# The second layer norm's output turned by DMA transposes of fp16 parts, and fp16 part products for Q, K and V

## Chip, cores and metric

One core of one Trainium2 chip. The metric is the device time of one execution of the program in microseconds (us), the median of several runs. Before the change it is 1558.5 us, the median of three runs (1556.65 to 1559.55).

## What is computed

A macaron block in float32 on 2 sequences of 2048 tokens with 256 features: half a feed-forward block, attention, half a feed-forward block, each behind a layer norm without weights.

```
h(x)  = relu(s0 * [x,-x] @ W0) * 2        # W0 entries +1 or -1, 512 x 1024
        relu(s1 * h @ W1) * 2             # 1024 x 1024, +1 or -1
        s2 * h @ W2                       # 1024 x 256, +1 or -1
x = x + 0.5 * h(layernorm(x))
x = x + attention(layernorm(x))           # 16 heads of 16, causal, then @ w_o.T + b_o
x = x + 0.5 * h(layernorm(x))
```

Inside the attention the three projections q, k and v are `layernorm(x) @ w.T` with 256 x 256 float32 weights. They are what the change is about.

## The kernel before

The 4096 tokens are cut into 8 chunks of 512. There are three phases. Phase A takes each chunk through the first feed-forward block, the second layer norm and the projections to q, k and v, which are stored to scratch in DRAM. Phase B is attention, pair of heads by pair of heads. Phase C is the output projection, the third layer norm and the second feed-forward block. The change touches phase A alone.

Every engine runs its own instruction list, written out by hand, and they meet at semaphores. An engine that waits for one semaphore holds up everything behind it in its list. In phase A one turn of the chunk loop does the following on TensorE (`chunk`, L1129):

- L1, the 1024 x 1024 layer of chunk c, tiles m = 0 to 2 (`pe_l1`, L427). Each of the 8 output tiles takes 16 matmuls of 512 columns, because the activations are kept as an fp16 high part and an fp16 low part;
- eight 128 x 128 transposes of the normalised rows of chunk c-1 (`pe_t2`, L742, by the helper `pe_transpose`, L403) into the PSUM tile `ffn_tr`;
- L1 tile m = 3;
- `pe_qk` (L748) and `pe_v` (L760) for chunk c-1: float32 matmuls of the turned rows `proj_in` with the turned weights `w_t`, 8 for Q and K with 512 columns and 8 for V with 256. The compiler emits two instructions for each float32 matmul, so the profile counts 16 and 16;
- L1 tiles m = 4 to 7, then L2 (`pe_l2`, L444, 64 matmuls of 256 columns), then L0 of chunk c+1 (`pe_l0`, L413, 32 matmuls of 512 columns).

The last chunk (c = 7) is written out apart from L1163 on. It has attention's first row-maximum items (`pe_early`, `dve_early`) put between its matmuls. `pe_qk` and `pe_v` of chunk 6 come there only after L1 and L2, and those of chunk 7 after them.

VectorE (`chunk` L964, `next_ln` L977) makes the low parts: `dve_hidden` (L509) subtracts the high part from each hidden tile. At the end of a turn it handles the 8 tiles of the next L0, the statistics of the second norm of chunk c (`dve_ln_stats(ln2, c)`), the statistics of the first norm of chunk c+2, and then finishes both norms (`dve_ln_finish`, L380), second norm first. The normalised rows are `ln2.xn` and `ln1.xn`. ScalarE makes the high parts (`act_hidden`, L493), copies the turned rows from PSUM to `proj_in` (`act_x2`, L771) and takes q, k and v out of PSUM (`act_qk` L777, `act_v` L785). `dve_qk` (L796) makes the low part of q and k.

The first norm of each chunk has already another way to the turned form: `act_x_rows` (L473) writes its fp16 high part by rows, `dve_x_rows` (L479) the low part, and `sp_turn_x` (L485) turns both with four DMA transposes issued from SyncE (SP), 128 tokens each. SP's list for phase A is at L832 to L847: in each turn it stores q, k and v of chunk c-1 and then turns the first norm's rows of chunk c+1. After chunk 3 it also loads the first two pairs of heads for phase B (`load_pair`).

GpSimd adds the output bias to the residual once `ln2.xn` is there (`add_bias`, L897).

Of the kernel before, what the change touches and what calls it, by code (L numbers as in the profile page):

```python
# [19 lines left out]
F32 = mybir.dt.float32  # L20
# [8 lines left out]
P = 128  # L29
# [16 lines left out]
QK_SCALE = 2.0 ** 3  # L46
M_SCALE = 2.0 ** 13
# [62 lines left out]
class PhaseASems:  # L110


    def __init__(self, new):
# [29 lines left out]
        self.wt = new("wt")  # L143

# [112 lines left out]
def build(nc, x, w_q, w_k, w_v, w_o, b_o, k0, k1, k2, s0, s1, s2, out):  # L257
# [8 lines left out]
    with ExitStack() as top:  # L266
# [374 lines left out]
        first_turn_after = sum(map(len, L1_FILLS[:3]))  # L641
        l2_after = sum(map(len, L1_FILLS))
        tr_after_turn = slots.index(0, first_turn_after)
# [72 lines left out]
        with ExitStack() as st:  # L716
# [13 lines left out]
            w_max = sbuf(st, "w_max", [P, 2], F32)  # L730
            w_amax = sbuf(st, "w_amax", [P, 2], F32)
            w_lim = sbuf(st, "w_lim", [P, 2], F32)
            w_pow = sbuf(st, "w_pow", [P, 2], F32)
            w_inv = sbuf(st, "w_inv", [P, 2], F32)
# [7 lines left out]
            def pe_t2(c, last=False):  # L742
                wait(nc.tensor, ln2.sem.xn, c + 1)
                if last:
                    wait(nc.tensor, sb.s_done, last_use(0, in_qk))
                pe_transpose(ln2, f.tr, se.t2_ps)

            def pe_qk(c, src, bank_free, fill=None):  # L748

                wait(nc.tensor, se.x2_t, c + 1)  # L750
                for j in range(2 * DT):
                    bank_free(j)
                    for kt in range(DT):
                        ins = nc.tensor.matmul(f.mm[:, j, :], w_t[:, j // DT, kt, j % DT * P:(j % DT + 1) * P],  # L754
                                               src[:, kt, :], start=(kt == 0), stop=(kt == DT - 1))
                    ins.then_inc(se.qk_ps, 1)
                    if fill:
                        fill()

            def pe_v(c, src, bank_free):  # L760

                for t in range(TPC):
                    if t % 2 == 0:
                        bank_free(t // 2)
                    for kt in range(DT):
                        ins = nc.tensor.matmul(f.acc[:, t // 2, t % 2 * D:(t % 2 + 1) * D], src[:, kt, t * P:(t + 1) * P],  # L766
                                               w_t[:, 2, kt, :], start=(kt == 0), stop=(kt == DT - 1))
# [3 lines left out]
            def act_x2(c, dst):  # L771
                wait(nc.scalar, se.t2_ps, c + 1)
                if dst is proj_in:
                    wait(nc.scalar, se.v_ps, c * 2)
                nc.scalar.activation(dst[:, :, :], f.tr[:, :, :], ACT.Copy).then_inc(se.x2_t, 1)

            def act_qk(c, js):  # L777
                for j in js:
                    if j == 0:
                        wait(nc.scalar, se.qk_st, c * 128)  # L780
                    wait(nc.scalar, se.qk_ps, c * 4 + j + 1)
                    nc.scalar.activation(qk_hi[:, j, :], f.mm[:, j, :], ACT.Copy,
                                         scale=qk_scale[:, j // DT:j // DT + 1]).then_inc(se.qk_hi, 1)

            def act_v(c):  # L785
                for j in range(2):
                    if j == 0:
# [4 lines left out]
                                         ACT.Copy).then_inc(se.v_ev, 1)  # L792
# [3 lines left out]
            def dve_qk(c, js):  # L796
                for j in js:
                    wait(nc.vector, se.qk_hi, c * 4 + j + 1)
                    nc.vector.scalar_tensor_tensor(out=qk_lo[:, j, :], in0=f.mm[:, j, :],
                                                   scalar=qk_scale[:, j // DT:j // DT + 1], in1=qk_hi[:, j, :],  # L800
# [3 lines left out]
            def _(sp):  # L804
# [36 lines left out]
                for i in range(QCH - 2):  # L841
                    store(1, i)
                    sp_turn_x(sp, f, i + QCH + 2)
                for i in range(2):
# [5 lines left out]
            def _(pool):  # L850
# [17 lines left out]
                pool.wait_ge(se.wmax, 2)  # L868
                nc.gpsimd.partition_all_reduce(w_amax[:, :], w_max[:, :], P, RMAX).then_inc(se.wamax, 1)
                pool.wait_ge(se.wamax, 1)  # L870
                pool.wait_ge(se.wscale, 2)
# [39 lines left out]
            def _(dve):  # L911
# [33 lines left out]
                for n in range(2):  # L945
# [15 lines left out]
                nc.vector.tensor_scalar(qk_scale[:, :], w_inv[:, :], QK_SCALE, None, ALU.mult).then_inc(se.wscale, 1)  # L961
# [15 lines left out]
                def next_ln(c):  # L977
# [4 lines left out]
                    dve_ln_finish(ln2, c, se.t2_ps)  # L982
# [3 lines left out]
                next_ln(0)  # L986
                with dve.Fori(1, NCH - 2) as c:
# [3 lines left out]
                dve_ln_finish(ln2, NCH - 2, se.t2_ps)  # L991
# [3 lines left out]
                for m in range(HT):  # L995
# [3 lines left out]
                    dve_hidden(f, c, [m], 1)  # L999
                dve_early(n)  # L1000
# [7 lines left out]
                dve_ln_finish(ln2, c, se.t2_ps)  # L1008
# [8 lines left out]
            def _(act):  # L1017
# [32 lines left out]
                act.wait_ge(se.wscale, 2)  # L1050
                act.wait_ge(se.vones, 1)
                chunk(1)
# [6 lines left out]
                act_hidden(f, c, range(0, 3), 1)  # L1059
                act_x2(c - 1, proj_in)  # L1060
                act_hidden(f, c, range(3, HT), 1)
# [3 lines left out]
                act_x2(c, proj_last)  # L1065
# [6 lines left out]
            def _(pe):  # L1072
# [56 lines left out]
                def chunk(c, first=False):  # L1129
# [15 lines left out]
                def fill_early():  # L1145
# [3 lines left out]
                    if n == tr_after_turn:  # L1149
                        wait(pe, se.x2_t, NCH - 1)  # L1150
# [14 lines left out]
                pe_l1(f, c, range(0, 3), l1_free(c, True), fill_early, fills=L1_FILLS)  # L1165
                wait(pe, sb.s_done, last_use(0, first_turn_after))
                pe_t2(c - 1)
                pe_l1(f, c, range(3, HT), l1_free(c, True), fill_early, fills=L1_FILLS)
# [359 lines left out]
```

## Time and profile before

| | us |
|---|---|
| median of three runs | 1558.5 |
| profiled execution, its own time | 1557.87 |
| profiled execution, span from first to last instruction | 1556.2 |
| TensorE busy | 1534.5 (99% of the span) |
| VectorE busy | 1121.3 (72%) |
| ScalarE busy | 840.4 (54%) |
| GpSimd busy | 193.6 (12%) |

Phase A takes from 0 to about 452 us, phase B to about 1190 us, phase C the rest. Busy time of TensorE counts overlapping matmuls once, so 99% says that it is hardly ever without work. How far apart matmuls start says how fast it works.

### The profile page before, as it was taken

The page shows a single profiled execution, that of the slowest core. Times are in us where ns is not written, and L with a number is a line of the kernel's source. Part 1 is how long each engine was busy: PE and PEld are TensorE (multiplying, and loading weights), DVE is VectorE, ACT ScalarE, POOL GpSimd, SP SyncE. Part 2 cuts the span into 40 slices and gives each one's busy share as a digit, 9 for nine tenths or more (in the row PEclk, how much of TensorE's full clock was granted, in tenths as well). Part 3 has the DMA queues.
Part 4 walks back from the last instruction along what each step waited for, and adds up shares of the span by engine and source line. Part 5 has one row for each costly group of instructions (what it writes and reads, how often), then busy time and mean ns, then how long its engine had stood idle before and what let it go on. Part 6 is the DMA issues. An engine that isn't in the chain of part 4 may idle for free.

```text
span 1556.2 us, 35447 instructions
## 1 busy us (share of the span) xinstructions
PE 1534.5 (99%) x14112; PEld 723.8 (47%) x14112; DVE 1121.3 (72%) x1616; ACT 840.4 (54%) x1703; POOL 193.6 (12%) x516
## 2 busy tenths in 40 slices
PE   6999999999999999999999999999999999999998
PEld 3555555555444333434334334333433555555554
DVE  6535543564769999999989999989996667666552
ACT  3223322322158888888888888888886222222221
POOL 4300000000111112121112212212220000000000
PEclk9999999999999999999999999999999999999999
DMA  5121023402040222211222211222220222211210
GB/s 172 28 68 54 13 68 89 113 13 67 1 116 23 63 70 62 70 43 45 61 70 63 83 54 54 67 83 69 65 76 22 82 68 74 74 53 55 81 27 14
DMA packets 146227, 96.39 MB, mean 62 GB/s; under 512 B 106544, under 2 KB 125616, under 8 KB 146096
## 3 DMA queue, kind: packets, MB, share of 16 engines
q1 hardware_dynamic: 146096, 94.54, 21.2%
q8 instruction: 94, 1.54, 0.4%
q14 instruction: 37, 0.30, 0.1%
HBM read 49.15 MB, written 37.75 MB: 56 GB/s over the span
## 4 chain that ended last, share of the span: by engine, by line
PE 97%; DVE 1%; ACT 1%; DMA 0%; issue 0%; DVEq 0%
PE ffn_mm L437 29%; PE ffn_mm L1312 18%; PE ffn_mm L1332 16%; PE ffn_mm L423 7%; PE ffn_acc L453 7%; PE ffn_acc L659 6%; PE ffn_tr L659 5%; PE ffn_mm L754 4%; PE ffn_acc L568 2%; PE ffn_acc L766 2%; DVE m_part L680 1%; PE ffn_tr L407 1%; PE ffn_tr L665 1%; PE ffn_acc L665 0%; ACT probs L1288 0%; DMA x_res<-L_attn_x 0%
## 5 line engine op out<-in xcount | busy, mean ns | idle before, releaser
L1288 ACT ACTIVATE probs<-ffn_mm 128x512 f32<-128x512 f32 (+1 forms) x960 | 471.1, 557 | 86.9 <-PE ffn_mm L1312 81.9
L680 DVE TENSOR_REDUCE m_part<-ffn_acc 128x2 f32<-128x1024 f32 (+1 forms) x348 | 369.9, 1063 | 32.8 <-PE ffn_acc L659 27.3
L1312 PE MATMUL ffn_mm<-qk 128*32 128x512 f16 (+7 forms) x5120 | 385.6, 353 | 3.6 <-ACT probs L1288 1.9
L437 PE MATMUL ffn_mm<-ffn_h1h,w 128*128 128x512 f16 x1024 | 388.3, 379 | 0.0
L437 PE MATMUL ffn_mm<-ffn_h1l,w 128*128 128x512 f16 x1024 | 388.1, 379 | 0.0
L680 DVE TENSOR_REDUCE m_part<-ffn_tr 128x2 f32<-128x1024 f32 (+2 forms) x292 | 308.4, 1056 | 37.2 <-PE ffn_tr L659 25.9
L503 ACT ACTIVATE ffn_h2h<-ffn_mm 128x512 f16<-128x512 f32 x128 | 76.4, 597 | 296.2 <-PE ffn_mm L437 294.7
L1332 PE MATMUL ffn_mm<-probs,v 128*32 128x512 f32 (+3 forms) x1920 | 236.0, 550 | 0.0
L1312 PEld LDWEIGHTS ffn_mm<-qk 66*32 66x32 f16 (+1 forms) x5120 | 134.9, 94 | 208.6 <-ACT probs L1288 92.1
L514 DVE SCALAR_TENSOR_TENSOR ffn_h2l<-ffn_mm,ffn_h2h 128x512 f16<-128x512 f32 x128 | 85.7, 686 | 166.8 <-ACT ffn_h2h L503 166.8
L437 PEld LDWEIGHTS ffn_mm<-ffn_h1h,w 128*128 128x128 f16 x1024 | 100.1, 98 | 118.9 <-issue 1.8
L437 PEld LDWEIGHTS ffn_mm<-ffn_h1l,w 128*128 128x128 f16 x1024 | 100.2, 98 | 117.9
L1288 ACT ACTIVATE ln_xn<-ffn_mm 128x512 f32<-128x512 f32 (+2 forms) x320 | 138.1, 509 | 25.8 <-PE ffn_mm L1312 25.0
L503 ACT ACTIVATE ffn_h1h<-ffn_mm 128x512 f16<-128x512 f32 x128 | 76.1, 597 | 131.2 <-PE ffn_mm L423 131.1
L659 PE MATMUL ffn_acc<-qk 64*128 64x512 f16 (+1 forms) x696 | 124.8, 353 | 1.2 <-DVE m_part L680 1.2
L423 PE MATMUL ffn_mm<-ffn_x,w 128*128 128x512 f16 x512 | 115.7, 385 | 2.4 <-DVE ffn_x L469 2.4
L453 PE MATMUL ffn_acc<-w,ffn_h2h 128*128 128x256 f16 x512 | 113.8, 273 | 0.3 <-DVE ffn_h2l L514 0.3
L453 PE MATMUL ffn_acc<-w,ffn_h2l 128*128 128x256 f16 x512 | 113.7, 272 | 0.0
L1241 POOL TENSOR_SCALAR_AFFINE_SELECT probs<-probs 128x256 f32<-128x256 f32 x192 | 77.7, 424 | 271.1 <-ACT probs L1288 271.1
L514 DVE SCALAR_TENSOR_TENSOR ffn_h1l<-ffn_mm,ffn_h1h 128x512 f16<-128x512 f32 x128 | 88.1, 691 | 32.1 <-ACT ffn_h1h L503 31.6
L659 PE MATMUL ffn_tr<-qk 64*128 64x512 f16 (+2 forms) x584 | 104.1, 351 | 0.0
L659 PEld LDWEIGHTS ffn_acc<-qk 64*128 64x128 f16 x696 | 36.7, 92 | 116.6 <-issue 112.9
(123 smaller groups left out, 1198.3 us busy)
## 6 DMA issues: line engine op xcount, KB each, us to landing
qk<-qk_scr SPq DMA_DIRECT2D x256, 64.0 KB, 2.7
ctx_scr<-ctx_out SPq DMA_DIRECT2D x64, 256.0 KB, 2.6
qk<-ctx_scr SPq DMA_DIRECT2D x56, 256.0 KB
v_scr<-v_pad SPq DMA_DIRECT2D x32, 256.0 KB, 3.7
v<-v_scr SPq DMA_DIRECT2D x16, 512.0 KB, 4.1
x_res<-L_attn_x SPq DMA_DIRECT2D x8, 512.0 KB, 3.8
qk_scr<-qk_hi SPq DMA_DIRECT2D x32, 128.0 KB, 1.9
qk_scr<-qk_lo SPq DMA_DIRECT2D x32, 128.0 KB, 1.9
```

The costliest lines, as they stand in the source:

```text
L423: ins = nc.tensor.matmul(f.mm[:, m % 4, :], w0[:, kt, m * P:(m + 1) * P], part[:, kt, :], start=(kt == 0 and part is f.xh), stop=(kt == DT ...
L437: ins = nc.tensor.matmul(f.mm[:, m % 4, :], w1[:, kt, m * P:(m + 1) * P], part[:, kt, :], start=(kt == 0 and part is f.h1h), stop=(kt == H ...
L453: ins = nc.tensor.matmul(f.acc[:, t // 2, t % 2 * D:(t % 2 + 1) * D], part[:, kt, t * P:(t + 1) * P], w2[:, kt, :], start=(kt == 0 and par ...
L503: nc.scalar.activation(dst[:, m, :], f.mm[:, m % 4, :], ACT.Relu).then_inc(hi, 1)
L514: nc.vector.scalar_tensor_tensor(out=dst[:, m, :], in0=f.mm[:, m % 4, :], scalar=0.0, in1=src[:, m, :], op0=ALU.max, op1=ALU.subtract).the ...
L659: ins = nc.tensor.matmul(s_ps[slot][:, h, 0:w], q_part(u, h, HEAD_ROWS[h], slice(t * P, (t + 1) * P)), k_part(u, h, HEAD_ROWS[h], slice(r ...
L680: nc.vector.tensor_reduce(m_part[u][:, t, :, r], s_ps[slot][:, :, 0:w], AX.X, ALU.max).then_inc(sb.s_done, 1)
L754: ins = nc.tensor.matmul(f.mm[:, j, :], w_t[:, j // DT, kt, j % DT * P:(j % DT + 1) * P], src[:, kt, :], start=(kt == 0), stop=(kt == DT - 1))
L1241: nc.gpsimd.affine_select(out=view, in_=view, compare_op=ALU.is_ge, fill=0.0, base=c0 - (kb - TPC * i) * P, pattern=[[0, 2], [1, w]], chan ...
L1288: nc.scalar.activation(prob_tile(g, j, slice(c0, CH)), st_ps[bank(k)][:, c0:CH], ACT.Exp, scale=scale_now).then_inc(se.exp_done, 1)
L1312: ins = nc.tensor.matmul(st_ps[bank(k)][c:c + 32, c0:CH], k_part(pair % 2, h, rows, slice(kb * P + c, kb * P + c + 32)), q_part(pair % 2, ...
L1332: ins = nc.tensor.matmul(ctx_ps[row:row + 32, c0:CH], v_buf[pair % 2][:, kb, h * 32:(h + 1) * 32], prob_tile(g, j, slice(c0, CH)), start=s ...
```

## The change

The turn of the second norm's rows leaves TensorE. For chunks 0 to 6, ScalarE writes an fp16 high part of `ln2.xn` times 2^8 by rows (`act_x2_rows`), VectorE the low part (`dve_x2_rows`), and SP turns both with four DMA transposes (`sp_turn_x2`) into `x2_parts`, which lies in the memory of `proj_in`. The three weights are scaled by a power of two and split once into fp16 high and low parts (`act_w_parts`, `dve_w_parts`). Each float32 matmul of `pe_qk` and `pe_v` becomes four fp16 ones: both parts of the rows with both parts of the weights, summed in PSUM. Chunk 7 keeps the TensorE transposes and the float32 matmuls.

On ScalarE and VectorE the new row steps stand right behind the hidden tile m = 0 of L1. On SP the turn stands ahead of the stores of the same chunk. The core of the diff:

```diff
+            def act_w_parts():
+                nc.scalar.wait_ge(se.w1, 2)
+                nc.scalar.wait_ge(se.wt, 4)
+                for n in range(3):
+                    nc.scalar.activation(w_parts[:, 0, n, :, :], w_t[:, n, :, :], ACT.Copy, scale=w_mul[:, n:n + 1]).then_inc(se.w_hi, 1)
+            def dve_w_parts():
+                for n in range(3):
+                    nc.vector.wait_ge(se.w_hi, n + 1)
+                    nc.vector.scalar_tensor_tensor(out=w_parts[:, 1, n, :, :], in0=w_t[:, n, :, :], scalar=w_mul[:, n:n + 1],
+                                                   in1=w_parts[:, 0, n, :, :], op0=ALU.mult, op1=ALU.subtract).then_inc(se.w_lo, 1)
+            def act_x2_rows(c):
+                wait(nc.scalar, ln2.sem.xn, c + 1)
+                wait(nc.scalar, se.x2_turned, c * 64)
+                nc.scalar.activation(x2_rows[:, :, 0, :], ln2.xn[:, :, :], ACT.Copy, scale=X_SCALE).then_inc(se.x2_hi, 1)
+            def dve_x2_rows(c):
+                wait(nc.vector, se.x2_hi, c + 1)
+                nc.vector.scalar_tensor_tensor(out=x2_rows[:, :, 1, :], in0=ln2.xn[:, :, :], scalar=X_SCALE,
+                                               in1=x2_rows[:, :, 0, :], op0=ALU.mult, op1=ALU.subtract).then_inc(se.x2_lo, 1)
+            def sp_turn_x2(sp, c):
+                wait(sp, se.x2_lo, c + 1)
+                wait(sp, se.v_ps, c * 2)
+                for t in range(TPC):
+                    sp.dma_start(x2_parts[:, :, t * P:(t + 1) * P], x2_rows[:, t, :, :].rearrange("p a d -> p (a d)"),
+                                 transpose=True).then_inc(se.x2_turned, 16)
+            def pe_qk(c, bank_free):
+                wait(nc.tensor, se.w_lo, 3)
+                nc.tensor.sem_inc(se.gate, 1)
+                wait(nc.tensor, se.x2_turned, c * 64 + 64)
+                for j in range(2 * DT):
+                    bank_free(j)
+                    for kt in range(DT):
+                        for w in range(2):
+                            for x in range(2):
+                                ins = nc.tensor.matmul(f.mm[:, j, :], w_parts[:, w, j // DT, kt, j % DT * P:(j % DT + 1) * P],
+                                                       x2_parts[:, x * DT + kt, :], start=(kt + w + x == 0), stop=(kt + w + x == 3))
+                    ins.then_inc(se.qk_ps, 1)
...
                 for i in range(QCH):
+                    sp_turn_x2(sp, i)
                     store(0, i)
                     sp_turn_x(sp, f, i + 2)
...
                 def chunk(c, first=False):
-                    dve_hidden(f, c, range(0, 4), 1)
+                    dve_hidden(f, c, range(0, 1), 1)
+                    if not first:
+                        dve_x2_rows(c - 1)
+                    dve_hidden(f, c, range(1, 4), 1)
...
                 chunk(0, first=True)
                 next_ln(0)
+                dve_w_parts()
...
                 def chunk(c, first=False):
-                    act_hidden(f, c, range(0, 3), 1)
+                    act_hidden(f, c, range(0, 1), 1)
+                    if not first:
+                        act_x2_rows(c - 1)
+                    act_hidden(f, c, range(1, 3), 1)
                     if first:
                         act_wt()
-                    else:
-                        act_x2(c - 1, proj_in)
...
                     if first:
                         pe_wt()
-                    else:
-                        pe_t2(c - 1)
                     pe_l1(f, c, range(3, 4), l1_free(c, first))
                     if not first:
-                        pe_qk(c - 1, proj_in, qk_free(c - 1))
-                        pe_v(c - 1, proj_in, v_free(c - 1))
+                        pe_qk(c - 1, qk_free(c - 1))
+                        pe_v(c - 1, v_free(c - 1))
```

`pe_v` is changed in the same way as `pe_qk`. The scaling constants get a third column for the V weights, with one more `tensor_reduce` and two more one-column operations on VectorE in chunk 0. In chunk 7 the row steps of chunk 6 stand behind tile m = 0 on ScalarE and VectorE too, and `pe_t2(c - 1)` with the wait ahead of it is gone from the middle of L1.

## Rows read from the trace of the kernel before

**Rows 1.** The page: busy us, share of the span, instructions

```profile
PE 1534.5 (99%) x14112; PEld 723.8 (47%) x14112; DVE 1121.3 (72%) x1616; ACT 840.4 (54%) x1703; POOL 193.6 (12%) x516
```

**Rows 2.** Chain of work that ended last, 159 to 220 us: start, us, what

```profile
165.47 6.91 PE ffn_mm L423 x32
172.38 10.36 PE ffn_mm L437 x48
182.74 0.87 PE ffn_tr L407 x8
183.61 3.45 PE ffn_mm L437 x16
187.06 6.87 PE ffn_mm L754 x16
193.93 3.45 PE ffn_acc L766 x16
197.38 13.81 PE ffn_mm L437 x64
211.20 7.05 PE ffn_acc L453 x64
```

**Rows 3.** Busy time by engine of one turn: stretch, length, PE, PEld, DVE...

```profile
172.38:225.15 52.77, 52.77 (x265) 28.84 (x264) 26.54 (x60) 15.88 (x26) 2.78 (x4) 1.00 0.19 50
```

**Rows 4.** VectorE's timeline: start, us, line, operation, count, idle before

```profile
179.10 1.38 DVE L399 TENSOR_SCALAR ln_xn<-x_res,ln_mv,ln_rstd 128x256 f32 x4
...
182.90 1.75 DVE L399 TENSOR_SCALAR ln_xn<-x_res,ln_mv,ln_rstd 128x256 f32 x4
184.57 1.87 DVE L514 SCALAR_TENSOR_TENSOR ffn_h2l<-ffn_mm,ffn_h2h 128x512 f16<-128x512 f32 x3
...
205.90 1.22 DVE L482 SCALAR_TENSOR_TENSOR ffn_xt<-ln_xn,ffn_xt 128x1024 f16<-128x1024 f32 x1 [0.25 <-ACT ffn_xt L477]
```

**Rows 5.** ScalarE's timeline of the same turn

```profile
204.82 1.05 ACT L477 ACTIVATE ffn_xt<-ln_xn 128x1024 f16<-128x1024 f32 x1
```

**Rows 6.** SP's timeline, and landing of L490 from 205 to 215 us

```profile
211.00 1.27 SPq L490 DMA_TRANSPOSE ffn_x<-ffn_xt  x1
...
DMA to landing us min/median/max: 2.5/2.5/2.5
```

**Rows 7.** SP's timeline and the page: plain stores of 128 KB

```profile
195.47 1.79 SPq L825 DMA_DIRECT2D qk_scr<-qk_hi  x4
...
qk_scr<-qk_hi SPq DMA_DIRECT2D x32, 128.0 KB, 1.9
```

**Rows 8.** Chain and VectorE's timeline in the first turn of the loop

```profile
59.92 6.91 PE ffn_mm L423 x32
...
78.73 1.87 DVE L514 SCALAR_TENSOR_TENSOR ffn_h2l<-ffn_mm,ffn_h2h 128x512 f16<-128x512 f32 x3
```

**Rows 9.** TensorE's timeline at the start, with its idle time

```profile
9.67 1.94 PE L407 MATMUL ffn_tr<-ident,ln_xn 128*128 128x128 f32 x8 [9.67 <-DVE ln_xn L399]
14.04 9.46 PE L423 MATMUL ffn_mm<-ffn_x,w 128*128 128x512 f16 x32 [2.44 <-DVE ffn_x L469]
```

**Rows 10.** Two stretches, L423 alone; granted clock third from the end

```profile
14.00:16.00 2.00, 1.96 (x5) 0.73 (x6) 1.00 1.19 280
...
168.00:170.00 2.00, 2.00 (x11) 0.88 (x9) 1.00 0.00 0
```

**Rows 11.** SP's timeline: the last of 34 loads for phase B

```profile
281.55 0.42 SPq L315 DMA_DIRECT2D v<-v_scr  x1
```

**Rows 12.** Last chunk: the chain, then VectorE's timeline

```profile
391.52 0.32 PE ffn_tr L659 x2
...
396.36 1.02 PE ffn_tr L407 x8
...
388.16 1.38 DVE L399 TENSOR_SCALAR ln_xn<-x_res,ln_mv,ln_rstd 128x256 f32<-128x256 f32 x4
...
390.39 0.68 DVE L680 TENSOR_REDUCE m_part<-ffn_tr 128x2 f32<-128x512 f32 x1
```

More of the change, by code:

```diff
@@ L46 @@
 QK_SCALE = 2.0 ** 3
+W_SCALE = 2.0 ** 10
 M_SCALE = 2.0 ** 13
@@ L143, in __init__ @@
         self.wt = new("wt")
+        self.w_hi = new("w_hi")
+        self.w_lo = new("w_lo")
+        self.x2_hi = new("x2_hi")
+        self.x2_lo = new("x2_lo")
+        self.x2_turned = new("x2_turned")
         self.t2_ps = new("t2_ps")
@@ L739, in build @@
             se = sa
[L742 to L745, printed above, removed]
-                pe_transpose(ln2, f.tr, se.t2_ps)
-            def pe_qk(c, src, bank_free, fill=None):
-                wait(nc.tensor, se.x2_t, c + 1)
+            x2_rows = w_in[:, 2:4, :, :].rearrange("p n t d -> p (n t d)").bitcast(F16).rearrange("p (t a d) -> p t a d", t=TPC, a=2)
+            x2_parts = proj_in[:, :, :].rearrange("p t n -> p (t n)").bitcast(F16).rearrange("p (a n) -> p a n", a=2 * DT)
@@ new lines, in pe_v @@
+            def pe_v(c, bank_free):
+                for t in range(TPC):
+                    if t % 2 == 0:
+                        bank_free(t // 2)
+                    for kt in range(DT):
+                        for x in range(2):
+                            for w in range(2):
+                                ins = nc.tensor.matmul(f.acc[:, t // 2, t % 2 * D:(t % 2 + 1) * D],
+                                                       x2_parts[:, x * DT + kt, t * P:(t + 1) * P],
+                                                       w_parts[:, w, 2, kt, :], start=(kt + w + x == 0), stop=(kt + w + x == 3))
+                    if t % 2 == 1:
+                        ins.then_inc(se.v_ps, 1)
@@ L751, in pe_qk, with pe_qk_last @@
+            def pe_qk_last(bank_free, fill):
+                wait(nc.tensor, se.x2_t, 1)
                 for j in range(2 * DT):
@@ L769, in pe_v, with act_x2_last, is_last, qk_mul @@
                         ins.then_inc(se.v_ps, 1)
[L771 to L775, printed above, removed]
+            def act_x2_last():
+                wait(nc.scalar, se.t2_ps, 1)
+                nc.scalar.activation(proj_last[:, :, :], f.tr[:, :, :], ACT.Copy).then_inc(se.x2_t, 1)
+            def is_last(c):
+                return isinstance(c, int) and c == NCH - 1
+            def qk_mul(c, j):
+                return qk_scale[:, j // DT:j // DT + 1] if is_last(c) else QK_SCALE / (X_SCALE * W_SCALE)
             def act_qk(c, js):
@@ L841, in _ @@
                 for i in range(QCH - 2):
+                    sp_turn_x2(sp, QCH + i)
                     store(1, i)
                     sp_turn_x(sp, f, i + QCH + 2)
+                sp_turn_x2(sp, NCH - 2)
                 for i in range(2):
@@ L944, in _ @@
                 dve.wait_ge(se.w_in, 64)
-                for n in range(2):
+                for n in range(3):
                     nc.vector.tensor_reduce(w_max[:, n:n + 1], w_in[:, n, :, :], AX.XY, ALU.max,
@@ L999, in _ @@
                     dve_hidden(f, c, [m], 1)
+                    if m == 0:
+                        dve_x2_rows(c - 1)
                 dve_early(n)
@@ L1058, in _ @@
                 c = NCH - 1
-                act_hidden(f, c, range(0, 3), 1)
-                act_x2(c - 1, proj_in)
-                act_hidden(f, c, range(3, HT), 1)
+                act_hidden(f, c, range(0, 1), 1)
+                act_x2_rows(c - 1)
+                act_hidden(f, c, range(1, HT), 1)
                 act_qk(c - 1, [0])
@@ L1164, in _ @@
                 wait(pe, f.sem.res, c * 2)
[L1165 to L1168, printed above, removed]
+                pe_l1(f, c, range(HT), l1_free(c, True), fill_early, fills=L1_FILLS)
                 wait(pe, sb.s_done, last_use(1, l2_after))
                 pe_l2(f, c, v_free(c - 1), fill_early)
-                pe_qk(c - 1, proj_in, lambda j: wait(pe, f.sem.l1_lo, c * HT + 5 + j))
-                pe_t2(c, last=True)
-                pe_v(c - 1, proj_in, v_free(c))
-                pe_qk(c, proj_last, lambda j: wait(pe, se.qk_lo, (c - 1) * 4 + j + 1), fill_early)
+                pe_qk(c - 1, lambda j: wait(pe, f.sem.l1_lo, c * HT + 5 + j))
+                pe_t2()
+                pe_v(c - 1, v_free(c))
+                pe_qk_last(lambda j: wait(pe, se.qk_lo, (c - 1) * 4 + j + 1), fill_early)
                 wait(pe, sb.s_done, last_use(1, len(AHEAD)))
-                pe_v(c, proj_last, lambda j: None)
+                pe_v_last()
         with ExitStack() as st:
```

58 lines of the change are left out of this document (30 added, 28 removed).

## The prediction, made before the changed kernel ran

> **What bounds the kernel now.** I read the page first: TensorE is busy 99% of the span and no other engine over 72% [rows 1]. A busy share does not show that nothing but TensorE matters, so I read the chain of work that ended last next. Through phase A it is TensorE without a break. One turn of the loop, from the start of L0 to the next start of L0, is 6.91 us of L0, 10.36 of L1 tiles 0 to 2, 0.87 of the eight transposes, 3.45 of tile 3, 6.87 of Q and K, 3.45 of V, 13.81 of tiles 4 to 7 and 7.05 of L2: 52.77 us [rows 2], the length at which TensorE is busy for all of a turn [rows 3]. So less work on TensorE pays one for one, as long as every operand is there when TensorE comes to it. The other engines' timelines say when that is. VectorE is busy half of a turn [rows 3], but its work is bunched right after L2, where both norms are made.
>
> **What TensorE gains.** The transposes go: 0.87 us in each of six turns. The products are hardly changed. 8 float32 matmuls of 512 columns take 6.87 us; the 32 fp16 ones that replace them have the shape of L0, whose 32 take 6.91. 8 float32 matmuls of 256 columns take 3.45; 32 fp16 ones are half of L2's 64, 3.52 [rows 2]. All four products cost what float32 costs, plus 0.11 us. The gain is 0.76 us a turn, 4.6 in six turns.
>
> **What it costs to have the rows turned in time.** I count from the start of L0 in the turn that starts at 165.47.
>
> - TensorE comes to Q and K after 6.91 + 10.36 + 3.45 = 20.72 us [rows 2].
> - VectorE finishes the second norm's rows at 179.10 + 1.38 = 180.5, and ScalarE can write their high part by about 181.6, since that operation is the one of L477, 1.05 us [rows 4, 5]. But VectorE's list goes on with the first norm to 184.6 and then tile 0 of L1, the first of three in 1.87 us, so some 0.60 [rows 4]. The low part starts at 185.17 and, as L482, takes 1.22: it ends at 186.4, 20.9 after the start of L0.
> - SP issues four DMA transposes, as in L490. There, the low part ends at 205.90 + 1.22 = 207.12, the fourth is issued at 211.00 and lands 2.5 later, at 213.5: 6.4 us from the end of the low part to the last landing [rows 4, 6]. SP is free: its last work was the previous turn, and after chunk 3 its loads for phase B end at 281.55, while the rows of chunk 4 would come 20.9 after that turn's start at 165.47 + 2 x 52.77 = 271.0, at 291.9 [rows 11]. Behind this turn in SP's list stand the stores of the same chunk, which need Q, K and V anyway.
> - TensorE can start Q and K at 20.9 + 6.4 = 27.3. It stalls for 6.6 us, and tiles 4 to 7, L2 and the next L0 stand behind the wait in its list; ScalarE and VectorE then wait for those.
>
> After the stall come Q and K 6.91, V 3.52, tiles 4 to 7 13.81, L2 7.05 = 31.29. The turn is 27.3 + 31.3 = 58.6 instead of 52.77: +5.8. Nothing refunds this, for VectorE's chain begins anew at each L2's end and never runs ahead.
>
> **The clock.** At the start TensorE sat idle for 9.67 us, and then its L0 took 9.46 us against 6.91 in the loop [rows 2, 9]. Five of those matmuls started in 2 us against eleven in the loop [rows 10]: that is 512 columns at 1.2 GHz against 2.4, though the granted clock is printed as 1.00 in both. The excess is 2.55 us, twelve matmuls that lose 0.427 - 0.216 = 0.211 each. I take it for each stall, as 6.6 us is nearer to 9.67 than to no gap. Bounds: 0, if that gap is too short to lower it, and 6.9 if all of Q and K (6.91 us) runs at half speed. With 2.55 a turn costs +8.4.
>
> The Trainium skill says of this in "TensorE: Matmul & The Clock Gate", section "HAM oscillation — how this bites in real kernels", that a TensorE waiting on a DMA between bursts falls back to half clock and pays for it in every round. By that rule it is my value and not 0; the only row is the one at the start.
>
> **The other parts.** First turn (rows of chunk 0): the DVE low parts of the weights stand ahead of everything there, three operations like L514, 1.87 us. Tiles 0 to 2 were at 78.73, 18.8 after L0's start at 59.92 [rows 8]; so 18.8 + 1.9 + 0.6 + 1.2 + 6.4 = 28.9, a stall of 8.2, and the turn is 28.9 + 31.3 + 2.55 - 52.8 = +9.9. ScalarE's three high parts lie in time that it has free. In chunk 0 a third maximum and two tiny operations add about a microsecond to VectorE while TensorE is in L1 tiles 1 and 2: hidden, unless VectorE were a tile late. ScalarE loses a copy of 1.02 us a turn and gains one of 1.05.
>
> Last chunk: the eight transposes of 1.02 go [rows 12]. Q and K come after L2, so the DMA is hidden. But on VectorE the low part (1.22 us, not before 390.6: the rows are ready at 389.5 and ScalarE's 1.05 follows) stands between tile 0 and the maximum at 390.39, which ends near 392.5 instead of 391.07, and TensorE's item at 391.52 in the same PSUM tile waits for it [rows 12]: about 1 us lost. Sum 0 (bounds -1 and +1.5).
>
> **Sum.** Five turns at +8.4 are 42, the first is 10, the last 0: +52. The profiled run's own time was 1557.87 us, 0.6 under the median of 1558.5, so 1610.
>
> The plain stores to compare with: four issues take 1.79 us and land 1.9 after issue, some 3.3 in all against 6.4 for the transposes [rows 7, 6]. The rows of this very form decide, so the sum has 6.4. The Trainium skill ("Advanced Engine Details and Errata", X-Bar Transpose) says that transposing DMAs run as fast as others. With 3.3 the stall would be 3.5 and the whole 6 x 3.1 = 19 us shorter, 1591.
>
> **Rivals.**
> - The clock holds: the stall comes, but matmuls start 0.216 us apart behind it. 1610 - 6 x 2.55 = 1595. For: no gap of this length lies in the loop to show a fall. Against: the start of the span. Chance 0.18.
> - The clock comes back later, by up to all of Q and K: 1610 to 1636, about 1625. Chance 0.07.
> - The transposes land as quickly as plain stores, so that the 1.3 us an issue of L490 is not met here: 1591. Against: L490 has the same shape [rows 6]. Chance 0.05.
> - The other side, **faster**: the rows are turned before TensorE comes. Its place is the wait ahead of `pe_qk`, its price minus 0.76 in six turns and about -0.9 in the last chunk: 1553. It decides where the low part is finished 6.4 us before 20.7, at 14.3; but the normalised rows themselves are there only at 15.0 (180.5 - 165.47). It would take a VectorE list other than this one. Chance 0.02. That the gain and a stall of under a microsecond cancel is 0.01.
>
> **Chances and range.** My own case has 0.67, with 1603 to 1618 by the size of the clock's term (about 1.5 to 3.8 a stall). The range reaches down to the clock that holds, 1593, and up to 1620; it leaves out most of the late clock, the plain-store speed and the other side, about 0.15. A measurement of this kernel can tell 0.2%, 3 us, from no change. Slower by more than that 0.97, within it 0.01, faster 0.02.
>
> **What would show it.** In the profile after: no L407 in the loop; the chain no longer all TensorE in phase A, but in each of six turns VectorE's norm operations, then the new low part, then the DMA of `sp_turn_x2`; TensorE idle about 6.6 us (8 in the first) ahead of the first Q matmul; a turn of 61 us instead of 52.77; Q and K taking 9.4 us for 32 matmuls rather than 6.9; phases B and C of unchanged length. A TensorE that does not wait ahead of Q, a low part that ends more than a microsecond from 20.9, or four transposes that land in another time than 6.4 would make the forecast wrong, each by itself.

## The result, and the profile after

The changed kernel takes 1614.9 us (median of 6 runs, 1612.7 to 1616.4) against 1557.7 for the kernel before (6 runs in the same session, 1556.7 to 1559.6): a ratio of 1.0368, with the interval 1.0358 to 1.0378. It is slower by 57 us where 52 were forecast, and inside the range. The profiled execution took 1615.2 us, its span is 1613.5, so the spans differ by 57.3.

Page of the changed kernel: busy time, and the granted TensorE clock in 40 slices. Against [rows 1] TensorE's share falls from 99 to 96%. In the clock row only the third slice prints less than 9, since a 9 stands for 0.90 and more; the stretches further down show the falls that a slice of 40 us hides.

```profile
PE 1546.4 (96%) x14280; PEld 722.0 (45%) x14280; DVE 1129.9 (70%) x1629; ACT 841.1 (52%) x1706; POOL 195.4 (12%) x516
PEclk9989999999999999999999999999999999999999
```

Chain of work that ended last, in the turn that answers to [rows 2]: start, length, what.

```profile
184.89 6.92 PE ffn_mm L431 x32
...
193.07 1.41 DVE ln_bn L358 x4
...
198.43 1.38 DVE ln_xn L407 x4
...
203.98 0.60 DVE ffn_h2l L522
204.58 1.14 DVE w_in L778
205.74 1.19 SPq L786
206.97 1.27 SPq L786
208.29 1.26 SPq L786
209.60 2.49 DMA proj_in<-w_in
212.13 9.86 PE ffn_mm L804 x32
222.00 3.49 PE ffn_acc L816 x32
225.49 13.81 PE ffn_mm L445 x64
239.30 7.05 PE ffn_acc L461 x64
246.35 3.67 PE ffn_mm L431 x17
```

No work of TensorE is on the chain between the end of L0 and the start of Q. In its place stand the two norms on VectorE, tile 0's low part (L522), the new low part (L778), and the four DMA transposes of L786: three issues, then the fourth with its landing, at 212.1. The turn is 246.35 - 184.89 = 61.46 us, not 52.77.

Waits of TensorE from 60 to 420 us (engine, line, what it waited for; total, times, longest). The six waits hold 40.9 us. In the kernel before, TensorE did not wait ahead of Q.

```profile
PE ffn_mm L804 <- DMA proj_in<-w_in: 40.9, 6, 8.3
```

Busy time by engine in stretches around that wait; the granted clock is the third number from the end. Behind the wait it is 0.50, the level of 1.2 GHz, and only five matmuls start in the first stretch and seven in the next, until it is 1.00 again and eleven start.

```profile
184.89:246.35 61.46, 54.94 (x290) 28.70 (x288) 27.26 (x60) 15.62 (x26) 2.78 (x4) 0.94 0.22 51
...
212.00:214.00 2.00, 1.86 (x5) 0.74 (x6) 0.00 (x0) 0.00 (x0) 0.00 (x0) 0.50 0.00 0
214.00:216.00 2.00, 2.00 (x7) 0.65 (x5) 0.00 (x0) 0.23 (x1) 0.00 (x0) 0.50 0.00 0
...
218.00:220.00 2.00, 2.00 (x11) 0.93 (x10) 0.69 (x1) 0.60 (x1) 0.00 (x0) 1.00 0.00 0
```

First turn, same chain (it answers to [rows 8]), with the weights' low parts in it:

```profile
60.17 6.92 PE ffn_mm L431 x32
...
79.06 1.99 DVE k_u L766 x3
81.05 0.60 DVE ffn_h2l L522
81.65 1.14 DVE w_in L778
...
86.66 2.50 DMA proj_in<-w_in
```

Where the 57.3 us are, from the start times of the same work in both traces:

| stretch | before | after | more |
|---|---|---|---|
| to the first L0 of the loop | 59.92 | 60.17 | 0.3 |
| first turn | 52.78 | 63.28 | 10.5 |
| five turns | 263.9 | 307.2 | 43.4 |
| last chunk, to attention's first context tile out | 84.8 | 85.8 | 1.0 |
| from the first to the 64th context tile | 734.6 | 736.9 | 2.2 |
| the rest | 360.2 | 360.2 | 0.0 |

### The profile page after: what moved, and what is told of

It is laid out like the page before. It is cut to its first block, busy times and chain, and to the rows that moved or that the text cites. A ratio compares the mean times of both kernels' runs of the same rounds, so it can differ in the third digit from the quotient of the medians.

```text
span 1613.5 us, 35842 instructions
## 1 busy us (share of the span) xinstructions
PE 1546.4 (96%) x14280; PEld 722.0 (45%) x14280; DVE 1129.9 (70%) x1629; ACT 841.1 (52%) x1706; POOL 195.4 (12%) x516
## 3 DMA queue, kind: packets, MB, share of 16 engines
q8 instruction: 95, 1.56, 0.4%
## 4 chain that ended last, share of the span: by engine, by line
PE 88%; DVE 5%; SPq 2%; ACT 2%; issue 1%; DMA 1%; DVEq 0%
PE ffn_mm L445 22%; PE ffn_mm L1392 17%; PE ffn_mm L1412 15%; PE ffn_acc L461 7%; PE ffn_mm L431 7%; PE ffn_acc L665 6%; PE ffn_tr L665 5%; PE ffn_mm L804 4%; PE ffn_acc L576 2%; PE ffn_acc L816 2%; SPq L786 1%; DVE ln_bn L358 1%; DVE ln_xn L407 1%; DMA proj_in<-w_in 1%; ACT probs L1368 1%
## 5 line engine op out<-in xcount | busy, mean ns | idle before, releaser
L445 PE MATMUL ffn_mm<-ffn_h1h,w 128*128 128x512 f16 x1024 | 388.3, 379 | 0.0
L445 PE MATMUL ffn_mm<-ffn_h1l,w 128*128 128x512 f16 x1024 | 388.1, 379 | 0.0
L522 DVE SCALAR_TENSOR_TENSOR ffn_h2l<-ffn_mm,ffn_h2h 128x512 f16<-128x512 f32 x128 | 85.5, 686 | 159.2 <-ACT ffn_h2h L511 159.2
L445 PEld LDWEIGHTS ffn_mm<-ffn_h1h,w 128*128 128x128 f16 x1024 | 100.1, 98 | 119.6 <-issue 1.8
L445 PEld LDWEIGHTS ffn_mm<-ffn_h1l,w 128*128 128x128 f16 x1024 | 100.2, 98 | 117.9
L1368 ACT ACTIVATE ln_xn<-ffn_mm 128x512 f32<-128x512 f32 (+2 forms) x320 | 137.9, 507 | 25.4 <-PE ffn_mm L1392 24.6
L522 DVE SCALAR_TENSOR_TENSOR ffn_h1l<-ffn_mm,ffn_h1h 128x512 f16<-128x512 f32 x128 | 88.2, 691 | 32.0 <-ACT ffn_h1h L511 31.5
L804 PE MATMUL ffn_mm<-proj_in,k_u 128*128 128x512 f16 x224 | 66.2, 469 | 40.9 <-DMA proj_in<-w_in 40.9
```

What stands on the lines that cost most here:

```text
L445: ins = nc.tensor.matmul(f.mm[:, m % 4, :], w1[:, kt, m * P:(m + 1) * P], part[:, kt, :], start=(kt == 0 and part is f.h1h), stop=(kt == H ...
L522: nc.vector.scalar_tensor_tensor(out=dst[:, m, :], in0=f.mm[:, m % 4, :], scalar=0.0, in1=src[:, m, :], op0=ALU.max, op1=ALU.subtract).the ...
L804: ins = nc.tensor.matmul(f.mm[:, j, :], w_parts[:, w, j // DT, kt, j % DT * P:(j % DT + 1) * P], x2_parts[:, x * DT + kt, :], start=(kt + ...
L1368: nc.scalar.activation(prob_tile(g, j, slice(c0, CH)), st_ps[bank(k)][:, c0:CH], ACT.Exp, scale=scale_now).then_inc(se.exp_done, 1)
```

## The experiments

The theory: the products cost nothing, the rows come too late, and the gap ahead of Q halves the clock behind it. The rivals were that the fp16 products themselves are dear, that the clock falls for another reason than the gap, and that the last landing is set by something other than VectorE's order and the DMA transposes.

### The products alone

TensorE transposes as before; the high and low parts are made from PSUM by `act_x2` and `dve_x2`; weights in parts and four fp16 products as in the change.

```diff
-                wait(nc.tensor, se.x2_turned, c * 64 + 64)
+                wait(nc.tensor, se.x2_lo, c + 1)
...
-                    sp_turn_x2(sp, i)
...
+                    else:
+                        pe_t2(c - 1)
```

> The fp16 products alone: the rows are turned by TensorE into PSUM as before, ScalarE and VectorE take the high and the low part out of PSUM, and the four products of Q, K and V are those of the change. No DMA turn. Theory of the late turn (the loss is TensorE's wait for the DMA turn and the half clock behind it): TensorE has 0.11 us more in a turn of the loop than the kernel before, and waits at most some tenths for the low part, so a turn is 52.9 to 53.5 us and the whole 1558 to 1563. Rival, the products (four fp16 products are dearer than the float32 pair, or a float32 matmul's two instructions ran closer together): Q and K stay at 9.9 us for 32 matmuls, a turn is 56 us and the whole above 1575.

Measured: 1564.2 us, ratio 1.0047 (1.003 to 1.0064), 1.2 above the range that was expected. A turn is 219.59 - 166.73 = 52.86 us. The profiled execution was the shortest of the four, 1561.05; its 3.2 us over the kernel before are 1.3 in the first turn, where Q waits 1.1 for VectorE's low part, 1.3 in attention, and tenths. The other 3 us of the median stand in no trace. Chain:

```profile
184.00 0.87 PE ffn_tr L415 x8
...
188.33 6.91 PE ffn_mm L799 x32
195.23 3.49 PE ffn_acc L811 x32
```

The products cost 6.91 + 3.49 against 6.87 + 3.45 [rows 2]. They are not where the 57 us are, and the rival's turn of 56 us did not come.

### The gap filled

28 matmuls of 512 columns into a free PSUM tile stand ahead of the wait.

```diff
+                if fill_wait:
+                    for _ in range(28):
+                        nc.tensor.matmul(f.tr[:, 0, :], ident_h[:, :], w1[:, 0, 0:CH], start=True, stop=True)
                 wait(nc.tensor, se.x2_turned, c * 64 + 64)
```

> The changed kernel, with 28 fp16 matmuls of 512 columns put on TensorE ahead of its wait for the turned rows, in each of the six turns. They write a PSUM tile that nothing reads. 28 x 0.216 = 6.0 us, less than the 6.5 us of the wait, so the rows come no sooner and no later. Theory that the half clock comes from the idle gap: the granted clock stays at 1.00, Q and K take 6.9 us instead of 9.9, a turn is 58.5 instead of 61.45, the whole 1614.9 - 6 x 2.95 = 1597. Rival, the slow Q and K belong to the products or to the tile in proj_in's memory: they stay at 9.9 us and the whole at 1615. Second rival: filler work holds the power or the queue of TensorE and delays Q: above 1615.

Measured: 1596.1 us, ratio 1.0247 (1.023 to 1.0265), 19 us under the change. The DMA lands no earlier, 27.2 us after L0's start (206.85 - 179.62), but Q and K take 7.08, not 9.86. Chain, then the stretch behind the wait, at clock 1.00:

```profile
179.62 6.92 PE ffn_mm L431 x32
204.31 2.49 DMA proj_in<-w_in
206.85 7.08 PE ffn_mm L807 x32
```

```profile
208.00:210.00 2.00, 2.00 (x11) 0.93 (x10) 0.58 (x1) 0.60 (x1) 0.00 (x0) 1.00 0.00 0
```

So TensorE's idleness in the gap causes the fall: useless work there, with the same landing, takes 9.86 - 7.08 = 2.78 us off a turn, 16.7 in six; attention, 2.8 us shorter here, is the rest (see below). The Trainium skill ("TensorE: Matmul & The Clock Gate", section "HAM oscillation — how this bites in real kernels") says that a TensorE that waits on a DMA between bursts restarts at half clock each time. All six gaps of the changed kernel, of 6.5 us and more, agree.

The 7.08 against 6.91 [rows 2] is no slower work. A 512-column matmul is recorded with 0.38 us, but in a stream the next one starts 0.216 later, and the chain counts a piece only from the end of the one before it. Behind a gap that overlap of 0.16 us has nothing to hide under. From the first matmul of Q to the first of V it is 6.92 us here and 9.70 in the changed kernel: again 2.78. So a turn of the loop comes out in full: the wait 6.5, the lost overlap 0.2 and the clock 2.8, less the gain of 0.8, are the 8.7 us.

### The low part ahead of the first norm

```diff
                     dve_ln_finish(ln2, c, se.x2_hi)
+                    dve_x2_rows(c)
                     dve_ln_finish(ln1, c + 2, f.sem.xl)
```

VectorE's low part is taken out behind tile 0; ScalarE's high part goes ahead of tile 0 as well.

> The changed kernel with the two row steps pulled forward: VectorE makes the low part right behind the second norm's rows and ahead of finishing the first norm of the next chunks, ScalarE the high part ahead of tile 0 of L1. Theory that the place in VectorE's list sets the landing: rows at 15.0 us after L0's start, high part at 16.1, low part at 17.3, landed at 23.7 instead of 27.2, so TensorE waits 3.0 us instead of 6.5. A turn is 55.0 us if the gap of 3 us does not lower the clock and 58 if it does; the first turn the same, since the weights' parts then stand behind the rows' part. The whole 1575 to 1594. Rival, the DMA turn itself sets the landing (its engines or queue are busy until then): the wait stays at 6.5 us, the whole at 1615.

Measured: 1587.5 us, ratio 1.0198 (1.0181 to 1.0215). The waits are 3.4 us each at most:

```profile
PE ffn_mm L804 <- DMA proj_in<-w_in: 20.1, 6, 3.4
```

The clock fell behind four of the six and stayed behind two. One of each, and a stretch behind the slow one, with the clock third from the end:

```profile
198.03 7.08 PE ffn_mm L804 x32
...
253.58 8.77 PE ffn_mm L804 x32
```

```profile
254.00:256.00 2.00, 2.00 (x7) 0.76 (x6) 0.00 (x0) 0.00 (x0) 0.00 (x0) 0.57 0.00 0
```

Waits 20.1, Q and K longer by 4 x 1.86 + 2 x 0.17 = 7.8, gain -4.6: 23.3 of the 25.5 us between the spans (1581.7 and 1556.2). The last chunk, with 2.8 us of waits for `m_part`, holds most of the rest. So the place in VectorE's list does set the landing: Q starts 24.1 us after L0 (198.03 - 173.94), 3.1 earlier than in the change, where 3.5 was expected.

### Two of the four DMA transposes

This kernel turns only half of each chunk's rows; the rest of `proj_in` is zero.

```diff
-                for t in range(TPC):
+                for t in range(TPC // 2):
```

The counts in the waits follow, and `proj_in` is set to zero once.

> The changed kernel, which turns by DMA only two of the four groups of 128 tokens in each of chunks 0 to 6; the other half of the turned rows is left at zero, so half of the projections of these chunks is left out of the computation. All matmuls stay. Theory: the turn costs 1.27 us an issue and then 2.5 to land, so the rows are there 2 x 1.27 = 2.5 us earlier, and the wait is 4.0 us instead of 6.5. If a gap of 4.0 us still lowers the clock, a turn is 58.9 and the whole 1600; if not, 55.9 and 1582. Rival, the landing time is bandwidth or a fixed latency and not issue: the wait falls by less than 1 us and the whole stays above 1608.

Measured: 1593.0 us, one run. Q starts 24.6 us after L0 (202.46 - 177.85), 2.6 earlier than with four. The chain shows one issue and the landing behind it:

```profile
198.69 1.19 SPq L786
199.92 2.50 DMA proj_in<-w_in
202.46 8.77 PE ffn_mm L804 x32
```

So each transpose costs its issue, 1.3 us, and only the last one's landing counts. The gap was 5.7 us in the first turn, followed by a Q of 9.30, and 3.9 in the other five, four of them followed by 8.77 and one by 7.08. That is why the whole came between the 1600 and the 1582 that were expected for a clock that always falls and one that never does.

### Q, K and V behind tile 5

Two more tiles of L1 (6.91 us) cover the stall; the order of the other engines follows.

```diff
-                    pe_l1(f, c, range(3, 4), l1_free(c, first))
+                    pe_l1(f, c, range(3, 6), l1_free(c, first))
```

> The changed kernel with Q, K and V of the chunk before put behind tile 5 of L1 instead of tile 3, on TensorE, ScalarE and VectorE alike. Nothing is taken out of the computation. Theory of the late turn: the rows still land 27.2 us after L0's start, and TensorE comes to Q now at 20.7 + 6.9 = 27.6, so it does not wait in the loop, but about 1.3 us in the first turn, where the rows land at 29.0. A turn is 52.77 - 0.76 = 52.0 us; the last chunk stays 0.7 longer than before. The whole 1558 - 4.6 + 1.3 + 0.7 = 1555.5 (1553.5 to 1558). Rival, the wait only moves (to the first norm's turn ahead of L0, which SP issues behind the stores, or to the PSUM banks that Q, K and L1 share): a turn of 54 us or more, the whole above 1566.

Measured: 1559.1 us (11 runs), ratio 1.0013 (1.0003 to 1.0023), 2 us over the kernel before and 1 over the range that was expected. The turn is what was expected, 218.03 - 166.05 = 51.98 us, 0.79 under the kernel before. Waits from 60 to 420 us, the largest two:

```profile
PE ffn_tr L665 <- DVE m_part L686: 1.5, 1, 1.5
PE ffn_mm L445 <- DVE ffn_h2l L522: 0.8, 1, 0.8
```

So all but 2 of the 57 us go with the place of the wait. But the five turns' 4.0 us are not in the total. The first turn is 0.8 longer (weights' low parts). From the last L0 of the loop to attention's first context tile it takes 88.1 us, not 84.8: 1.0 of it is what the change has there too, with the 1.5 us wait, and some 2.3 go with a clock that in the profiled execution fell for 6.8 us right there, though in the 60 us before it TensorE had never waited for more than 0.8 us:

```profile
456.00:458.00 2.00, 2.00 (x21) 0.49 (x16) 1.01 (x4) 1.57 (x3) 0.00 (x0) 0.50 0.85 191
```

And attention, whose code is the same, takes 736.6 us from first to last context tile, not 734.6. That is taken up below.

### The product of the low parts left out

As the last, but both low parts are never multiplied with each other: three products of four, so the smallest term of each result is missing.

```diff
-                        for w in range(2):
-                            for x in range(2):
+                        for w, x in ((0, 0), (0, 1), (1, 0)):
...
```

> As the kernel with Q, K and V behind tile 5, but the product of the low parts of rows and weights is left out of Q, K and V in chunks 0 to 6: three fp16 products for each float32 one. Theory: with the wait gone TensorE's work sets the time again, and each chunk loses 8 matmuls of 512 and 8 of 256 columns, 8 x 0.216 + 8 x 0.109 = 2.6 us; seven chunks 18.2 us, the whole 1537. Rival, the turn is bound by VectorE's chain by now: less than half of that comes back, the whole above 1546.

Measured: 1543.1 us, ratio 0.9911 (0.9894 to 0.9927); a turn is 211.41 - 161.73 = 49.68. By count it is 51.98 - 8 x 0.216 - 8 x 0.109 = 49.4. The whole was expected at 1537 and missed that by 6 us: 0.3 a turn, 1.8 in all, lie in the loop, and 3.6 are what the four products behind tile 5 had missed already (1559.1 for 1555.5). Against those it is 16.0 us, of 18.2 expected, so the turn is still set by TensorE's work.

### No wait at all

Behind tile 5, low part ahead of the first norm, and the last chunk's row steps behind tile 2.

```diff
-                    if m == 0:
+                    if m == 2:
                         dve_x2_rows(c - 1)
```

> Q, K and V behind tile 5 of L1, all four products, and the row steps moved: in the loop VectorE's low part ahead of finishing the first norm (and ScalarE's high part ahead of tile 0), in the last chunk both behind tile 2 instead of tile 0. Theory: the rows land at 23.7 us in every turn and TensorE comes to Q at 27.6, so that the first turn loses its wait too, 1.3 us, and in the last chunk the maximum that waited for the low part is on time, 1.5 us. The whole 1558 - 4.6 - 0.9 = 1552.5 (1551 to 1555), and the chain through phase A is TensorE alone again. Rival: the low part waits 1.1 us for ScalarE and pushes the first norm and tile 0 of L1 back, and TensorE waits for a PSUM bank instead: no faster than with the row steps where they were.

Measured: 1564.6 us, ratio 1.0052 (1.0038 to 1.0066), not the 1552.5 expected: the rival happened. Chain of one turn:

```profile
291.64 1.56 DVE w_in L778
...
296.31 0.61 DVE ffn_h2l L522
296.97 7.08 PE ffn_mm L445 x32
```

The new operation (1.56 us there, 1.14 in the place of the change) pushes the first norm back, and with it tile 0's low part, which frees the PSUM tile that tile 4 of L1 is written to: `L445` now waits for it, 6.1 us over six turns, 2.5 of them in the first turn, where the clock fell behind the wait and two tiles ran 8.77 instead of 6.91. The turn is 52.88. In the last chunk the step behind tile 2 did work: L0 to Q is 51.17 us, not 52.77, and the 1.5 us wait is gone.

The same with three products:

> As the kernel without waits (Q, K and V behind tile 5, row steps moved), and again the product of the low parts is left out of Q, K and V in chunks 0 to 6. Theory: 18.2 us below the kernel without waits, 1534.5. Rival: less than 15 us below it, because a wait of VectorE or of the turn comes back in the shorter turn.

Measured: 1549.1 us, ratio 0.9946 (0.9931 to 0.9961), 15.5 us under the same order with four products (18.2 expected) and 6 us slower than the three products without this order. It has the same wait of 6.1 us, and attention is 1.8 longer, in a profiled execution whose clock fell once more there.

### Where the list stands

Between experiments attention took 734.1 to 737.8 us with the same instructions. Most of the differences are single stalls of about 1 us, some of which the profile puts down to nothing ("issue"), as here after the change, from 1038 to 1052 us:

```profile
PE ffn_acc L665 <- issue: 1.3, 1, 1.3
```

I asked whether the length of TensorE's list ahead of attention sets them. Semaphore increments that nobody waits for, at the head of the list, shift all of it. First the kernel before with 98 of them, then the kernel with Q behind tile 5 with 56:

```diff
+                for _ in range(98):
+                    pe.sem_inc(se.gate, 1)
                 pe.wait_ge(se.consts, 2)
```

> The kernel before, with 98 semaphore increments put at the head of TensorE's list, where it waits 9.7 us for the first rows anyway (98 x 0.051 = 5.0 us). Nothing else is changed; TensorE's later instructions only stand 98 places further on in its program, about as far as the change moved them. Phase B is not touched by the change, yet its stretch from the first to the last ctx_out took 736.9 us after against 734.6 before, by stalls of about a microsecond at a few fixed places of TensorE's list, put down to issue. Theory that the place of the code sets these stalls: phase A is unchanged, the stalls move to the places that they have in the changed kernel (the 19th, 22nd, 43rd and 47th interval), phase B takes 735 to 737 and the whole 1 to 3 us more than the kernel before. Rival, the stalls come from what phase A does or by chance: time and places as in the kernel before, 1557 to 1558.

> The kernel with Q, K and V behind tile 5, and 56 semaphore increments at the head of TensorE's list, as many places as the filler matmuls of e2_filler took, whose phase B was the shortest. Theory of the place of the code: phase B falls from 736.6 to about 734.1 and the whole from 1559.1 to 1556.5, a little under the kernel before. Rival: no difference, 1559.

Both expectations have slips. The loop stands once in the list, so the filler took 28 places there and not 56; and the first one numbers the intervals of attention one higher than the table below.

Measured: 1566.7 us, ratio 1.0059 (1.0045 to 1.0073), for the first; 1555.8 (11 runs), 0.9990 (0.9981 to 0.9999), for the second. Start of TensorE with 98 and with 120 increments (the latter in a kernel further down):

```profile
15.98 1.94 PE L407 MATMUL ffn_tr<-ident,ln_xn 128*128 128x128 f32 x8 [15.98 <-issue]
```

```profile
19.34 1.94 PE L415 MATMUL ffn_tr<-ident,ln_xn 128*128 128x128 f32 x8 [19.34 <-issue]
```

An increment takes (19.34 - 15.98) / 22 = 0.15 us, and the 98 stand as far apart, (15.7 - 0.9) / 97. The trace records each with 51 ns alone, which is the 0.051 of the expectation:

```profile
L1074 PEldq EVENT_SEMAPHORE  x98: 51/51/51, 0.9 to 15.7; - x98
```

98 of them last longer than the 9.67 us that TensorE waits there [rows 9] and delay the whole kernel by 6.4 (first L0 of the loop at 66.31, not 59.92). That I had missed; 56 still fit. The other 2.9 us are attention's: 737.6, not 734.6. And with 56 increments attention takes 733.9 where the same kernel without them takes 736.6. I took the 63 intervals from one context tile out to the next (ScalarE's timeline) and compared each with its median over all 14 kernels. Those longer by over 0.3 us, with the excess in us:

| kernel | instructions more in TensorE's list than before, counted from the code | stalled intervals |
|---|---|---|
| before | 0 | 29th 0.9, 50th 1.0 |
| three products | 48 | 26th 0.7, 50th 2.5 |
| three products, no wait | 48 | 26th 0.7, 50th 4.1 (with a fall of the clock) |
| the change | 80 | 18th 0.8, 21st 0.7, 46th 1.2 |
| low part first | 80 | 18th 0.8, 21st 0.3, 46th 0.4 |
| two DMA transposes | 80 | 42nd 0.7, 46th 0.7, 50th 0.4 |
| Q behind tile 5 | 80 | 18th 0.7, 21st 0.7, 42nd 0.4, 46th 1.0, 49th 0.6 |
| no wait at all | 80 | 18th 0.7, 42nd 1.0, 46th 0.9, 50th 0.3 |
| the products alone | 96 | 18th 0.9, 42nd 1.2 |
| before, 98 increments | 98 | 18th 0.8, 21st 1.0, 46th 1.2, 49th 0.5 |
| gap filled | 108 | 13th 0.9, 41st 0.5 |
| Q behind tile 5, 56 increments | 136 | 13th 0.8, 41st 0.9 |
| the same, last chunk's step moved (below) | 136 | 13th 0.9, 41st 0.5 |
| three products of that, 120 increments (below) | 168 | 41st 0.4 |

Kernels with different phases A but nearly the same list length stall in the same group of places, though not in every one of them, and one kernel at two lengths does not. So the length of the list moves the stalls. There is one trace of each kernel, so how much of the choice within a group is chance stays open. Why the stalls come (how code is fetched, for example), no run here shows.

### The last chunk's step moved as well

As Q behind tile 5 with 56 increments, and in the last chunk the row steps behind tile 2 instead of 0. Then the same with three products and 120 increments.

> As r10_tile5_shift, and in the last chunk the two row steps of chunk 6 stand behind tile 2 of L1 instead of tile 0. Theory: the maximum of the second item is on time again and TensorE does not wait for it, so that from the last L0 to Q takes 51.2 us instead of 52.8: 1.6 us less than r10_tile5_shift, 1555. Rival: the low part is in the way of another maximum there, and the last chunk stays at 52.5 or more.

> As r11_tile5_last_shift, with the product of the low parts of rows and weights left out of Q, K and V in chunks 0 to 6, and 120 increments at the head so that the later code stands at the same place. Theory: 18 us less than r11_tile5_last_shift, 1537, with phase B at 734 to 735. Rival: phase B above 736 in spite of the place, the whole 1540 or more.

Measured for the first: 1554.6 us (11 runs), ratio 0.9978 (0.9969 to 0.9987). It keeps all four products and is 3 us faster than the kernel before, 60 us faster than the change. Of the 3 us some 1.0 is attention's (733.6 us, not 734.6), which the length of the list gives and not the products. The step moved is worth 1.2 us (1.6 expected); this profiled execution, too, has the clock's fall of 6.8 us at the start of attention. Its longest wait in phase A (that for `m_part` is gone):

```profile
PE ffn_mm L445 <- DVE ffn_h2l L522: 0.8, 1, 0.8
```

For the second: 1547.9 us, not the 1537 expected, ratio 0.9942 (0.9929 to 0.9956), 5 us slower than three products without it. Attention shortened as wanted (733.3, not 736.0), but 120 increments started TensorE at 19.34 instead of 9.38. This is the same oversight as with 98.

## Why the prediction was right, and where it was off

**The stall.** Right in each step. The low part ended 205.72 - 184.89 = 20.8 us after L0's start (20.9 forecast), the transposes landed 6.4 later, Q started at 27.24 (27.3). The landing time came from the same form of operation [rows 6]. Halving the number of transposes took 2.6 us off, two issues. The Trainium skill ("Advanced Engine Details and Errata", X-Bar Transpose) says that transposing DMAs are as fast as regular ones. This case's traces do not agree: four took 6.4 us to the last landing, where four plain stores of the same size, which go to DRAM, took some 3.3 [rows 7]. With the stores' time the waits would have been 3.1 us shorter, an estimate, and they were not.

**TensorE's gain.** Right: the products cost 0.08 us a turn more than float32 (0.11 forecast), and the 0.87 of transposes went. With the stall covered, a turn is 0.79 shorter (0.76).

**The clock.** Right in kind: filling the gap took the term away. The term "2.55 us, twelve matmuls" was too small: 9.86 - 6.91 = 2.95. Both numbers hold the lost overlap of 0.16 us; the clock itself took 2.78, 13 matmuls' worth at 0.211, and 2.39, 11 of them, in the row at the start. Over six turns the 0.4 are 2.4 us of the 5 by which the total was off. That row measured how long the clock stayed down once, under other work, so that it came this near is in part luck.

**The first turn.** +10.5 against 9.9; 0.4 of it is again the clock's term, 0.12 the low parts (1.99, not 1.87).

**The last chunk.** "Sum 0" was the term mis-sized the other way. The transposes' 1.02 us went, but the wait for `m_part` was 1.5 us instead of 1.0. ScalarE's high part was on time: the low part started 444.79 - 430.69 = 14.1 us after the last L0 of the loop, where 390.6 - 376.56 = 14.0 was forecast. But it took 1.64, not 1.22. To attention's first context tile it makes +1.0; 0.5 of that is the wait less the transposes, the rest stays open. Last chunk, waits, and the two operations ahead of the maximum:

```profile
PE ffn_tr L665 <- DVE m_part L686: 1.5, 1, 1.5
```

```profile
443.70 1.06 ACT w_in L773
444.79 1.64 DVE w_in L778
446.43 0.61 DVE m_part L686
447.18 0.39 PE ffn_tr L665 x2
```

**Phases B and C.** "Of unchanged length" failed by 2.2 us in phase B: the change made TensorE's list longer, and where the shift was made alone, attention changed by as much. Phase C held to 0.1 us.

**The rivals.** The clock holds (1595): it does if the gap is filled, 1596. Transposes as fast as stores (1591): no. Faster: the prediction said that it would take another VectorE list (its 1553 counts from the median of 1558.5; from 1557.87, where its 1610 starts, it is 1552.4). Moving the low part forward was not enough (still a 3.4 us wait), and with the wait covered it was harmful. What was enough was TensorE's order, which the prediction had not weighed.

## What to carry to other kernels

A chain of small steps on other engines replaces a short step on the bounding one only if its landing, counted from the last operand, lies before the place where the bounding engine needs it; if it does not, move that place behind work already ready, before shortening the chain. A stall of several microseconds ahead of matmuls was charged twice here, once as a gap and once as the slow matmuls behind it, so cover it whole or fill it. When a change of a microsecond is judged, look whether untouched stretches changed length too.

## What was not expected

- The clock fell behind four gaps of six at 3.2 to 3.4 us, four of five at 3.9, the one of 5.7, and six of six at 6.5 us and more. It also fell behind both gaps of 2.5 us (first turn of the two kernels "no wait at all"), in three kernels (two DMA transposes, Q behind tile 5, last chunk's step moved) at the start of attention with no wait over 0.8 us close before it, and behind a stall of 2.2 us inside attention in one kernel of the two that have it. The length of the gap alone does not tell; shorter gaps are rather a lottery than free. Q and K took 8.73 to 8.77 us behind the short gaps with a fall, 9.30 behind 5.7, and 9.86 behind the long ones.
- The 1.00 that is printed for the clock at the start of the span [rows 10] is no measurement: the trace's first clock record begins at 18.83 us, just where matmuls go from 0.427 us apart to 0.216. There the spacing says the level, not the printed number.
- Semaphore increments on TensorE take 0.15 us each, though recorded with 0.05.
- The length of an instruction list moves 1 us stalls about in code that is the same: 733.3 to 737.8 us for one phase, up to 0.3% of the kernel. That is as much as the change's own gain could be.
